# Two-layer attention and expert kernel: scores and maxima issued head by head over rings of four and three banks, batch work in half-bank pieces

## What is computed

```python
def attention(x):                       # b, l = 4, 2048; 16 heads of 16
    q, k, v = heads(x @ Wq), heads(x @ Wk), heads(x @ Wv)
    s = einsum('bhqd,bhkd->bhqk', q, k) / 4      # + alibi bias in layer one
    s = where(causal, -inf, s)
    return einsum('bhqk,bhkd->bhqd', softmax(s), v) @ Wo
x = x + attention_a(norm(x)); x = x + experts(norm(x))
x = x + attention_b(norm(x)); x = x + experts(norm(x))
```

## Time and profile before

| | us |
|---|---|
| median of 2 runs | 5716.87 |
| lowest, highest | 5715.9, 5717.84 |
| the profiled execution's own time | 5713.13 |
| its span in the profile | 5711.3 |

### The profile page before, as it was taken

The page is one execution under the profiler, slowest core; times in us unless marked ns, Lnnn a source line. Parts: engine busy times, 40 slices in busy tenths (PEclk is TensorE's granted clock), DMA queues, the critical chain, the costliest instruction groups (busy, mean ns, idle before and its releaser), DMA issues. The chain is left out here.

```text
span 5711.3 us, 100322 instructions
## 1 busy us (share of the span) xinstructions
PE 4624.8 (81%) x40833; PEld 2451.1 (43%) x40833; DVE 2905.7 (51%) x3519; ACT 2814.5 (49%) x6099; POOL 1076.2 (19%) x1428
## 2 busy tenths in 40 slices
PE   4688888888888877888968888888888888888477
PEld 2344434443444333446834433444344443443266
DVE  1656555655656555553045655555555555555000
ACT  1355555555555555553235555555555555555121
POOL 4111002110221034210032320332033301100101
PEclk8789879997999788888978987899788987878688
DMA  3322222221322133313533222332123212220154
GB/s 126 51 49 47 43 52 65 73 58 33 74 64 68 25 94 90 75 49 120 168 96 76 76 51 55 82 84 68 25 74 89 79 37 51 61 42 9 48 170 150
DMA packets 238725, 406.56 MB, mean 71 GB/s; under 512 B 29324, under 2 KB 153484, under 8 KB 225164
## 3 DMA queue, kind: packets, MB, share of 16 engines
q1 hardware_dynamic: 235192, 391.76, 27.5%
q0 software_dynamic: 3072, 8.39, 0.5%
HBM read 264.25 MB, written 121.50 MB: 68 GB/s over the span
## 5 line engine op out<-in xcount | busy, mean ns | idle before, releaser
L948 DVE TENSOR_REDUCE part_max<-ps_p 128x2 f32<-128x1024 f32 (+3 forms) x2560 | 2675.7, 1063 | 1949.9 <-PE ps_p L762 1540.5
L636 ACT ACTIVATE probs<-ps_r 128x512 f32<-128x512 f32 (+3 forms) x5120 | 2455.0, 533 | 1833.2 <-PE ps_r L739 1024.4
L739 PE MATMUL ps_r<-q_stack,k_stack 54*128 54x512 f32 (+3 forms) x5120 | 1285.5, 498 | 684.1 <-ACT probs L636 659.4
L789 PE MATMUL ps_acc<-probs,v_head 128*17 128x256 f32 x18432 | 1508.4, 449 | 0.7 <-ACT probs L636 0.7
L762 PE MATMUL ps_p<-k_stack,q_stack 52*128 52x512 f32 (+3 forms) x5120 | 1121.9, 434 | 127.5 <-DVE part_max L948 105.3
L739 PEld LDWEIGHTS ps_r<-q_stack,k_stack 54*128 54x128 f32 x5120 | 516.4, 197 | 1558.5 <-ACT probs L636 1133.4
L789 PEld LDWEIGHTS ps_acc<-probs,v_head 128*17 128x17 f32 x18432 | 604.0, 112 | 781.5 <-issue 462.5
L762 PEld LDWEIGHTS ps_p<-k_stack,q_stack 52*128 52x128 f32 x5120 | 540.3, 207 | 166.4 <-DVE part_max L948 138.5
L535 POOL TENSOR_TENSOR r<-r 128x4 f32<-128x4 f32 x36 | 7.2, 200 | 1847.8 <-DVE r L929 1847.8
L822 PE MATMUL ps_r<-xT,wqkv 128*128 128x512 f32 x512 | 285.9, 690 | 2.7 <-ACT xT L654 2.7
L831 PE MATMUL ps_r<-wo,bk 128*128 128x256 f32 x512 | 149.2, 444 | 134.2 <-POOL bk L574 134.2
(11 more groups left out here) (90 smaller groups left out, 2222.8 us busy)
## 6 DMA issues: line engine op xcount, KB each, us to landing
probs<-w_dram SPq DMA_DIRECT2D x60, 1024.0 KB, 7.8
q_stack<-parts SPq DMA_DIRECT2D x384, 128.0 KB
k_stack<-parts SPq DMA_DIRECT2D x384, 128.0 KB
parts<-pa SPq DMA_DIRECT2D x128, 256.0 KB, 2.1
parts<-pb SPq DMA_DIRECT2D x128, 256.0 KB, 2.4
o_sums<-acc_sb SPq DMA_DIRECT2D x1024, 17.0 KB
bk<-o_sums SPq DMA_DIRECT2D x64, 256.0 KB
bk<-recips SPq DMA_DIRECT2D x64, 256.0 KB
```

The source lines that it names most:

```text
L636: act.activation(probs[:, at % PBUF, u, 0:QW - q0], ring(i + u)[:, q0:QW], ACT.Exp)\
L739: mm[u] = pe.matmul(ring(i + u)[:, q0:QW], ks[s][r, kb * P:(kb + 1) * P], qs[s][r, qt * QW + q0:(qt + 1) * QW], start=True, stop=True)
L789: mm = pe.matmul(ps_acc[tile:tile + DH + 1, first:e % 2 * D + D], v_head[:, beta % 2, kb, 2 * p + u, :], probs[:, at % PBUF, u, lo - q0:to ...
L948: dve.tensor_reduce(part_max[:, :, qb, kc], ps_p[:, at % 2 * 2:at % 2 * 2 + 2, 0:w], AX_X, ALU.max)\
```

## The change

Five things change together.

1. The two heads are issued singly. In a step TensorE now has: score of head 0, maximum tile of head 1, score of head 1, maximum tile of head 0. Every one has its own wait, and its own semaphore tells of it (`s_mm[u]`, `p1_mm[u]`).
2. The banks are dealt anew: `ps_r` has four (`RING = 4`), `ps_p` three (`P1_RING = 3`), both used a bank at a time.
3. VectorE reduces each head's tile by an instruction of its own; ScalarE waits per head.
4. Jobs come in halves of a bank (256 columns): 4 `xt`, 8 `qk`, 4 `v`, 4 `y` per chunk, with as many ScalarE and GpSimd pieces; the tables `front` and `back` give them new steps.
5. `PBUF` goes from 12 to 8 blocks, and the experts' `hid`, `xs_sb` and `xsT` get memory of their own; the experts' banks are swapped to match the new rings. Value rounds stay at four blocks, the evacuations of `ps_acc` come one step earlier.

```diff
-RING = 3
-PBUF = 12
+RING = 4
+P1_RING = 3
+PBUF = 8
...
         for u in range(4):
-            t = at + 20 + 7 * u
-            out += [(t, ("qk", f, c, u)), (t + 2, ("sw", f, c, u)), (t + 3, ("sp", f, c, u)), (t + 9, ("st", f, c, u))]
-        out += [(at + 48, ("v", f, c, 0)), (at + 55, ("v", f, c, 1))]
+            t = at + 18 + 6 * u
+            out += [(t, ("qk", f, c, 2 * u)), (t + 2, ("qk", f, c, 2 * u + 1)),
+                    (t + 4, ("sw", f, c, u)), (t + 5, ("sp", f, c, u)), (t + 11, ("st", f, c, u))]
+        out += [(at + 42 + 2 * i, ("v", f, c, i)) for i in range(CH)]
...
+        for i in range(CH):
+            out += [(at + 34 + 6 * i, ("y", r, c, i)), (at + 36 + 6 * i, ("ba", r, c, i))]
...
-                act.wait_ge(ring_mm, i + 2)
                 for u in range(2):
+                    act.wait_ge(s_mm[u], at + 1)
                     act.activation(probs[:, at % PBUF, u, 0:QW - q0], ring(i + u)[:, q0:QW], ACT.Exp)\
...
-            def scores(g, n):
+            def score(g, n, u):
...
-                pe.wait_ge(ring_used, i - 1)
-                mm = [None, None]
-                diagonal = kb >= 4 * qt
-                for u in range(2):
-                    r = slice(HALF * u, HALF * u + ROWS)
-                    mm[u] = pe.matmul(ring(i + u)[:, q0:QW], ks[s][r, kb * P:(kb + 1) * P],
-                                      qs[s][r, qt * QW + q0:(qt + 1) * QW], start=True, stop=True)
+                pe.wait_ge(ring_used, i - RING + 1)
+                r = slice(HALF * u, HALF * u + ROWS)
+                mm = pe.matmul(ring(i)[:, q0:QW], ks[s][r, kb * P:(kb + 1) * P],
+                               qs[s][r, qt * QW + q0:(qt + 1) * QW], start=True, stop=True)
...
-            def unit(g, n):
+            def unit(g, n, u):
...
-                if at >= 2:
-                    pe.wait_ge(p1_used, at - 1)
+                if at >= P1_RING:
+                    pe.wait_ge(p1_used, at - P1_RING + 1)
...
                 elif kind == "qk":
-                    half, proj = divmod(i, 2)
+                    u, j = divmod(i, 2)
+                    half, proj = divmod(u, 2)
                     lo = proj * D + half * P
                     for k in range(KD):
-                        mm = pe.matmul(to, wqkv[:, k, lo:lo + P], xT[:, k, :], start=(k == 0), stop=(k == KD - 1))
+                        mm = pe.matmul(to[:, 0:D], wqkv[:, k, lo:lo + P], xT[:, k, j * D:(j + 1) * D],
+                                       start=(k == 0), stop=(k == KD - 1))
...
-                    scores(g, n)
-                    if g + 1 < NG:
-                        unit(g + 1, n)
+                    for u in range(2):
+                        score(g, n, u)
+                        if g + 1 < NG:
+                            unit(g + 1, n, 1 - u)
...
-                dve.wait_ge(p1_mm, 2 * at + 2)
-                dve.tensor_reduce(part_max[:, :, qb, kc], ps_p[:, at % 2 * 2:at % 2 * 2 + 2, 0:w], AX_X, ALU.max)\
-                    .then_inc(p1_used, 1)
+                for u in (1, 0):
+                    dve.wait_ge(p1_mm[u], STEPS * g + n + 1)
+                    dve.reduce_max(part_max[:, u, qb, kc:kc + 1], p1_bank(g, n, u)[:, 0:w], AX_X).then_inc(p1_used, 1)
```

More of the change, by code:

```diff
@@ L66 @@
 LAST_GROUP = {3: 3, 2: 6, 1: 8, 0: 9}
[L67 to L70 removed]
+EVAC_STEP = {3: 17, 2: 29, 1: 37}
+LATE_EVAC = 1
+C_HI, C_LO = 34, 6
 def front(f):
@@ L274, in build @@
         qk_split = sem("qk_split")
-        ring_mm = sem("ring_mm")
+        s_mm = [sem(f"s_mm{u}") for u in range(2)]
+        job_mm = sem("job_mm")
         ring_used = sem("ring_used")
-        p1_mm = sem("p1_mm")
+        p1_mm = [sem(f"p1_mm{u}") for u in range(2)]
         p1_used = sem("p1_used")
@@ L725, in _ @@
             mm.then_inc(bias_mm, 1)
[L727 removed]
+            def score(g, n, u):
                 qt, kb, q0 = BLOCK[n]
[L729 to L730 removed]
+                i, s = PLACE[("s", g, n, u)], g % SLOTS
+                if n == 0 and u == 0:
                     pe.wait_ge(rows_in[1], 32 * (g + 1))
[L732 removed]
+                if n == FIRST_LO and u == 0:
                     pe.wait_ge(rows_in[0], 32 * (g + 1))
[L734 to L749 removed]
@@ L752, in unit @@
+                mm.then_inc(s_mm[u], 1)
+            def unit(g, n, u):
                 qb, kc, w = UNIT[n]
-                at, s = STEPS * g + n, g % SLOTS
-                if n == 0:
+                at, s = p1_place(g, n, u), g % SLOTS
+                if n == 0 and u == 1:
                     pe.wait_ge(stack_in[s], stack_count(g))
-                if at >= 2:
-                    pe.wait_ge(p1_used, at - 1)
-                mm = [None, None]
-                diagonal = kc == qb // 4
-                for u in range(2):
-                    r = slice(HALF * u, HALF * u + MAX)
-                    mm[u] = pe.matmul(ps_p[:, at % 2 * 2 + u, 0:w], qs[s][r, qb * P:(qb + 1) * P],
-                                      ks[s][r, kc * QW:kc * QW + w], start=True, stop=True)
@@ L764, in unit @@
-                if diagonal:
-                    for part in range(2):
-                        for u in range(2):
-                            r = slice(HALF * u, HALF * u + HALF)
-                            lo = w - P + HALF * part
-                            mm[u] = pe.matmul(ps_p[:, at % 2 * 2 + u, lo:lo + HALF], mk[r, part, :], id64[r, :],
-                                              start=False, stop=True, skip_group_check=True)
-                for u in range(2):
-                    mm[u].then_inc(p1_mm, 1)
+                if at >= P1_RING:
+                    pe.wait_ge(p1_used, at - P1_RING + 1)
@@ new lines, in unit @@
+                r = slice(HALF * u, HALF * u + MAX)
+                mm = pe.matmul(p1_bank(g, n, u)[:, 0:w], qs[s][r, qb * P:(qb + 1) * P], ks[s][r, kc * QW:kc * QW + w],
+                               start=True, stop=True)
+                if kc == qb // 4:
+                    r = slice(HALF * u, HALF * u + HALF)
+                    for part in range(2):
+                        lo = w - P + HALF * part
+                        mm = pe.matmul(p1_bank(g, n, u)[:, lo:lo + HALF], mk[r, part, :], id64[r, :], start=False,
+                                       stop=True, skip_group_check=True)
```

157 lines of the change are left out of this document (76 added, 81 removed).

## The result

The changed kernel takes 5323.26 us (median of two runs, 5300.85 to 5345.67) against 5716.87: 0.9311 of the time before, 95% interval 0.9143 to 0.948, so faster by about 7%. The forecast was 5144 us in a range of 4880 to 5500. The direction is right and the time lies inside the range, but the gain is 394 us where 573 were forecast, and the likeliest case's own range (5030 to 5270) missed it.

What follows compares the result with a forecast made beforehand. The prediction took a loop of TensorE and ScalarE waiting for each other as the bound. Rounds 55, jobs 7.5, odd waits 1.5 and clock 3 made 67 us per group against 76.1, giving 5144 us, range 4880 to 5500.

Steps and rivals of the forecast that it cites:

- the loop term: Rounds of a group at full clock, without jobs, paced by VectorE's reductions: 55 us per group, 60 before.
- sum of five reductions per round: In VectorE's loop, five reductions must end before a round's eighth tile is issued: 5 x 0.60 + 0.1 us.
- I take 3 us per group: TensorE's low clock in the groups: costs 3 us per group after the change instead of 5 (bounds 0 and 5).
- the 71 us: Mean group of the kernel before at full clock, taken from groups at nearly full clock of 67.9 and 74.0 us.
- jobs in halves: Half-bank jobs on TensorE: cost falls from 11 to 7.5 us per group (bounds 5 and 11).
- TensorE's slack of 10 us: TensorE's spare time per group after the change, 55 - 45 us, in which jobs could partly hide.
- A: Rival: a mask matmul waiting for its score holds back the other half's tile in diagonal steps; 5400 us, chance 0.26.
- B: Rival: clock always full in groups, jobs hidden but for 5 us per group; 4860 us, chance 0.13.
- C: Rival: same within 2%, VectorE's loop catches every job and the clock stays as low; 5615 us, chance 0.10.
- D: Rival: no two row halves run together on TensorE, a full step takes 1.32 us; 6110 us, slower, chance 0.09.
- the 45 us per group: TensorE's own need per group for scores, maximum tiles, masks and value rounds: 45 us, rounded up.

Runs made afterwards that it cites:

- four tile banks: The changed kernel with three banks for scores and four for maximum tiles, the experts' banks swapped to match: 5085.58 us.
- lighter reductions: The changed kernel with VectorE reducing only every second column, half of the comparisons for the row maxima left out: 4820.63 us.
- the filler: Head 0's score computed twice in three steps of four, in groups seven and eight of each eight: changed kernel 5269.17 us; on two-block rounds 5019.71 us.
- the whole-bank run: The changed kernel with the jobs of the kernel before (whole banks, old steps): 5346.52 us, 0.9354 of the kernel before.
- two-block rounds: The changed kernel with value rounds of two blocks every two steps instead of four every four: 4970.42 us; same edit on the kernel before: 5232.99 us.

## Why the prediction was right and where it was wrong

**Right: what goes and what comes.** The scores' wait for exponentials is gone (659.4 us to 3.4 on matmuls), and the tiles' wait for VectorE took its place. Wide reductions are 0.68 us long and start 0.60 apart (0.69 and 0.60 forecast). Full rounds take 5.7 to 5.95 us (5.9 to 6.0 forecast), and a value round keeps its 1.65 or 1.85. The changed kernel's order of time, starts of value rounds at full clock:

```profile
3206.19 1.92 PE L794 MATMUL ps_acc<-probs,v_head 128*17 128x256 f32 x32
...
3211.90 1.92 PE L794 MATMUL ps_acc<-probs,v_head 128*17 128x256 f32 x32
...
3217.85 1.71 PE L794 MATMUL ps_acc<-probs,v_head 128*17 128x256 f32 x24
```

These are 5.71 and 5.95 us apart. That VectorE's loop decides is shown by the runs: four tile banks, shorter bursts and lighter reductions each take the time down by 238 to 503 us.

**Wrong: the loop term, 55 instead of 56.9.** The sum of five reductions per round left out VectorE's other work. (It also adds up to 5.90 us for a full round, not the 5.95 written there, so the true sum of the ten rounds is nearer 54.5.) Where a half of the maxima is complete, three small operations stand between two tiles' reductions. TensorE and VectorE in the changed kernel:

```profile
3234.96 0.32 PE L769 MATMUL ps_p<-k_stack,q_stack 52*128 52x128 f32 x1 [0.56 <-DVE part_max L953]
```

```profile
3233.66 0.22 DVE L959 TENSOR_REDUCE negmax<-part_max 128x16 f32<-128x64 f32 x1
3233.92 0.17 DVE L965 CAST cp<-negmax 128x16 fp32r<-128x16 f32 x1
3234.13 0.17 DVE L967 TENSOR_TENSOR cp<-negmax,cp 128x16 fp32r<-128x16 f32 x1
3234.22 1.68 DVE L953 TENSOR_REDUCE part_max<-ps_p 128x1 f32<-128x512 f32 x4
```

From 3233.66 to 3234.22 VectorE reduces no tile; the last tile of the round waits those 0.56 us with TensorE empty, and the round takes 6.53 us. It comes twice per group, 1.1 us of the 1.9. The remaining 0.8 I can't place.

**Wrong in size: "I take 3 us per group" for the clock.** Measured 5.4, and a clock of 0.88 and 0.90 instead of "0.90 to 0.93". The clock did rise, as was argued: in the 14 groups with almost no jobs from 0.78 to 0.85 in the mean (the seventh group alone went the other way, 0.83 to 0.77). But the level stayed low. The argument was that stretches between value rounds hold the same matmuls in less time, with no gap of 0.48. The gap is gone, but the pace is not: once the reserve is used up, a step takes 1.20 us by VectorE as it took 1.21 by ScalarE. That too little matmul work lowers the clock is what the filler shows with both signs; that VectorE's pace is what thins the work out is what lighter reductions and four tile banks show, with 1.00 and 0.98 in the same groups. The clock's cost before was put too low as well (5 instead of 8.3), so the gain by it came out at 2.9 (2.1 by the straight lines), with 2 forecast. Both that 5 and the 11 for jobs hang on the 71 us taken for the mean group at full clock from two groups; less its cost of clock the mean group takes 67.8.

**Wrong: "jobs in halves", 11 to 7.5.** This is the largest part of the missing gain when terms are compared as differences. Jobs and odd waits cost 7.5 before and 8.1 after, where 11 and 9 were taken. The premise was that TensorE's slack of 10 us would hide them. It hides next to nothing more than before, and the whole-bank run shows that their size is not the reason: jobs of either size give the same time. That a job lets VectorE drain its three tiles, which then has to be fed anew, is my guess and can't be all of it: with half of each reduction, and with two-block rounds, the groups with jobs still take 66.2 and 68.5 us where those almost without take 49.7 and 53.3. Why jobs cost as much as they do stays open. The recorded count of them also mixes two means: its 5.7 us per group hold for the six groups of eight that have jobs, and over all eight they are 4.3, so that by its own count the term was 6 and not 7.5. As differences the forecast had 5 + 2 + 2 = 9 us per group and the traces have 3.4 + 2.9 - 0.6 = 5.7; times 62, and with 12 outside the groups, that is the 367 us measured. A half projection moreover takes 1.06 us from its start to the next matmul, not 0.95.

**The rivals.** A (strict order in the array) falls. TensorE in a diagonal step of the changed kernel, where the program's order is score 0, mask, tile 1, score 1, mask, tile 0:

```profile
1002.31 0.39 PE L750 MATMUL ps_r<-q_stack,k_stack 54*128 54x256 f32 x1
1002.32 0.50 PE L769 MATMUL ps_p<-k_stack,q_stack 52*128 52x512 f32 x1
1002.54 0.23 PE L756 MATMUL ps_r<-id,mk 64*128 64x64 bf16 x2
1002.61 0.47 PE L769 MATMUL ps_p<-k_stack,q_stack 52*128 52x512 f32 x1
1002.66 0.28 PE L750 MATMUL ps_r<-q_stack,k_stack 54*128 54x256 f32 x1
```

Tile 1 starts at 1002.32 beside score 0, ahead of the masks. Tile 0 starts at 1002.61 in the half that is free, ahead of score 1 at 1002.66, which stands before it in the program but needs the half that tile 1 holds. The rule of the Trainium skill ("TensorE: Matmul & The Clock Gate", Part 3, "The mechanism"), that matmuls start in program order, does not hold for these row halves either; only the measured time happens to lie between the forecast and A's, by chance nearer to A's. B falls by the clock (5.4 us instead of none) and the jobs. C had rounds and clock about right (57 and 5, measured 56.9 and 5.4), but put 12.5 us for jobs and odd waits, where 8.1 were measured. D falls with the pairs 0.02 us apart.

## What to carry to other kernels

Count the reserve in front of every engine that a ring feeds, against the longest burst that TensorE runs without feeding it; here a bank more was worth 238 us and a burst half as long 353, and the two together no more than the second. The burst half as long alone (484 us on the kernel before) was worth at least about as much as the whole change, which removed the most visible wait. When one wait is removed, compute the pace of what is late next: if it is the same per step (1.20 for 1.21 here), the gain is only in the reserve, and TensorE's clock rises little (0.86 to 0.89 in the whole groups here). A low clock can go with a steady trickle of half-array matmuls in an engine that the profile shows as busy (0.77 with 67.2 of 68.2 us), so look at the clock in all stretches without jobs before costing it.

## What was not expected of the hardware

More matmul work made the kernel faster: 30 repeated scores in each took the 14 groups from a mean of 64.0 us to 60.7, and their clock from 0.85 to 0.97.

Pairs of half-array matmuls that nothing blocks run faster than the 0.33 us per pair that I had read from the earlier trace rows. TensorE in the changed kernel after a job:

```profile
1009.75 0.50 PE L750 MATMUL ps_r<-q_stack,k_stack 54*128 54x512 f32 x1
1009.76 0.73 PE L769 MATMUL ps_p<-k_stack,q_stack 52*128 52x512 f32 x2
1010.10 0.63 PE L750 MATMUL ps_r<-q_stack,k_stack 54*128 54x512 f32 x2
1010.34 0.39 PE L769 MATMUL ps_p<-k_stack,q_stack 52*128 52x512 f32 x1
1010.57 0.39 PE L750 MATMUL ps_r<-q_stack,k_stack 54*128 54x512 f32 x1
```

The first pair takes 0.34 us to the next start (1009.76 to 1010.10), the following ones 0.24 and 0.23. TensorE's own need was therefore less than the 45 us per group of the prediction, and the slack larger than assumed; the jobs cost 8.1 us per group all the same.
